# Attention's values product with v held and the probabilities moved, in an early-fusion block

## What is computed

```
q = rope(X @ Wq + bq);  k = rope(X @ Wk + bk);  v = X @ Wv + bv      # 12 heads of 16
scores = einsum('bqhd,bkhd->bhqk', qh, kh) / sqrt(16), causal mask
weights = softmax(scores)
out = einsum('bhqk,bkhd->bqhd', weights, vh).reshape(B, 48, 192)
return out @ Wo + bo
```

## Time and profile before

| | us |
|---|---|
| median of 3 runs | 270.15 (269.02 to 271.35) |
| profiled execution | 271.69 |
| its span in the trace | 268.7 |
| PE busy | 243.2 (91%) |
| DVE busy | 171.9 (64%) |
| ACT busy | 131.2 (49%) |
| POOL busy | 120.2 (45%) |

### The profile page before, as it was taken

How to read it: one execution, slowest core, us unless ns; L and a number is a source line. 1 busy time by engine, 2 the same in 40 slices (tenths; PEclk the granted TensorE clock), 3 DMA queues, 4 the chain that set the end, 5 groups by cost and what they waited for, 6 DMA issues and landing times.

```text
span 268.7 us, 5694 instructions
## 1 busy us (share of the span) xinstructions
PE 243.2 (91%) x2077; PEld 195.3 (73%) x2082; DVE 171.9 (64%) x534; ACT 131.2 (49%) x349; POOL 120.2 (45%) x132
## 2 busy tenths in 40 slices
PE   7887979999899989999989999999999999999920
PEld 2656666666677667667558989899998989898910
DVE  7467349879887977878765585574828293763310
ACT  0214374878597767765345455352717172541300
POOL 8055212451675276342652064462808172647380
PEclk9999999999999999999999999999999999999975
DMA  7960089700001211263014977757585768432241
GB/s 226 357 209 2 1 192 324 324 2 4 32 33 34 99 39 33 69 180 91 32 47 107 271 168 157 171 133 179 82 216 76 178 139 177 91 33 27 27 41 14
DMA packets 24491, 31.03 MB, mean 115 GB/s; under 512 B 3149, under 2 KB 21521, under 8 KB 24336
## 3 DMA queue, kind: packets, MB, share of 16 engines
q1 hardware_dynamic: 16928, 20.77, 28.5%
q0 software_dynamic: 5904, 8.48, 15.8%
q10 hardware_dynamic: 1632, 1.42, 1.9%
HBM read 20.34 MB, written 10.08 MB: 113 GB/s over the span
## 4 chain that ended last, share of the span: by engine, by line
PE 59%; DVE 12%; DMA 8%; issue 6%; POOL 6%; ACT 5%; ACTq 1%; POOLq 0%; SPq 0%; DVEq 0%
PE bank L718 12%; PE scores L709 5%; PE scores L702 5%; PE scores L703 5%; PE scores L710 5%; PE scores L706 4%; PE bank L421 3%; DMA slots<-rows,slot 2%; PE bank L407 2%; PE bank L687 2%; POOL slots L1382 2%; PE bank L492 2%; PE bank L443 2%; DMA early<-in_patches 2%; DMA keys<-slots 2%
## 5 line engine op out<-in xcount | busy, mean ns | idle before, releaser
L1431 POOL DMA_INDIRECT out_rows<-blank,tok x32 | 55.0, 1718 | 63.4 <-DVE blank L1309 56.4
L932 ACT ACTIVATE blank<-scores 128x480 f32<-128x480 f32 (+1 forms) x33 | 18.4, 560 | 58.8 <-PE scores L710 58.8
L1382 POOL DMA_INDIRECT slots<-rows,slot x24 | 24.6, 1024 | 32.7 <-DVE rows L1186 12.0
L718 PE MATMUL bank<-w_sb,blank 128*120 128x192 f32 x224 | 37.7, 326 | 0.0
L718 PEld LDWEIGHTS bank<-w_sb,blank 128*120 128x120 f32 x224 | 36.2, 183 | 0.1
L1320 DVE TENSOR_TENSOR blank<-blank,scores 128x480 f32<-128x480 f32 (+1 forms) x33 | 21.0, 639 | 19.3 <-ACT blank L932 19.2
L1309 DVE SCALAR_TENSOR_TENSOR blank<-bank,keys,blank 120x192 f32<-120x192 f32 x32 | 11.5, 412 | 28.5 <-DMA out_rows<-blank,tok 22.8
L702 PE MATMUL scores<-z0h,wah 128*128 128x480 f32 x64 | 25.4, 397 | 0.0
L709 PE MATMUL scores<-z,wbh 128*128 128x480 f32 x64 | 24.5, 383 | 0.3 <-DVE z L1305 0.3
L703 PE MATMUL scores<-z0h,wal 128*128 128x480 f32 x64 | 24.3, 379 | 0.0
L706 PE MATMUL scores<-z0l,wah 128*128 128x480 f32 x64 | 24.3, 379 | 0.0
(11 more groups left out here) (197 smaller groups left out, 532.2 us busy)
## 6 DMA issues: line engine op xcount, KB each, us to landing
early<-in_w SPq DMA_DIRECT2D x8, 512.0 KB, 5.0
early<-in_w SPq DMA_DIRECT2D x16, 256.0 KB, 6.2
w_sb<-in_w SPq DMA_DIRECT2D x8, 384.0 KB, 4.0
slots<-blank POOLq DMA_DIRECT2D x1, 3030.0 KB, 14.0
keys<-slots SPq DMA_DIRECT2D x8, 378.8 KB, 5.1
early<-in_patches SPq DMA_DIRECT2D x1, 1152.0 KB, 9.8
h_all<-in_hinit SPq DMA_DIRECT2D x1, 864.0 KB, 11.1
tokw_all<-in_tokw ACTq DMA_DIRECT2D x1, 576.0 KB, 4.1
```

Of the source, the lines that this page charges most:

```text
L718: mm = pe.matmul(o, hT[:, m, c * CR:(c + 1) * CR], w2_sb[:, par, m, :], start=(m == 0), stop=(m == MH - 1))
L932: act.activation(sg[:, m % 2, cols], up_bank[2 * (m % 2)][:, cols], ACT.Silu).then_inc(s_silu, 1)
L1382: pool.indirect_dma_start(out=slots, out_offset=bass.IndirectOffsetOnAxis(ap=slot[:, 2 * t + k:2 * t + k + 1], axis=0), in_=rows[:, t, :], ...
L1431: pool.indirect_dma_start(out=out, out_offset=bass.IndirectOffsetOnAxis(ap=tok[:, e, c:c + 1], axis=0), in_=yw[:, c, :], in_offset=None, b ...
```

## The change

`values(j)` holds v and moves the probabilities. For each image (48 moved columns) and pair of heads, `vbd` without its ones (128 rows, 32 columns) is held, and the result, 32 features x 48 tokens, goes to partitions 32 (p mod 4) on of bank 6: pairs of heads 0 to 3 in columns 0 to 111, 4 and 5 in columns 128 on. Then eight matmuls hold a block of ones (128 x 32, new tile `ones_sb`) and move `pT`'s 112 columns: they give each token's sum for a head, repeated over the head's 16 partitions, in columns 256 to 511; pairs of heads 4 and 5 are written twice, so that all 128 partitions are filled. `divide(j)` takes the reciprocal of all of these (128 partitions x 4 x 48) and multiplies twice, straight into `oT0` (128 x 96) and `oT1` (64 x 96), and counts `s_oT`. `turn_attention`, `copy_attention`, `att` and their semaphore waits go.

```diff
--- before.py
+++ after.py
@@ -198,13 +198,13 @@
         kk = sb("kk", [P, 2 * P])
         qT_sb = sb("qT_sb", [P, 2 * 3 * GTOK])
         qT = qT_sb[:, :].rearrange("p (a n k) -> p a n k", a=2, n=3)
-        vbd = sb("vbd", [P, 2, 2, HEADS // 2, 2, HD + 1])
+        vbd = sb("vbd", [P, 2, 2, HEADS // 2, 2, HD])
+        ones_sb = sb("ones_sb", [P, 2, HD])
         sm = sb("sm", [P, HEADS * S])
         mx = sb("mx", [P, HEADS])
         pr = sb("pr", [P, 2, HEADS, HALF])
         pT = sb("pT", [P, 2, HEADS // 2, WIDE])
-        rden = sb("rden", [P, HEADS])
-        att = sb("att", [P, 2, D])
+        rden = sb("rden", [P, 4, S])
         oT0 = sb("oT0", [P, 2, GTOK])
         oT1 = sb("oT1", [D1 + 1, 2, GTOK])
         st2 = sb("st2", [P, 6])
@@ -484,19 +484,18 @@
                     t = projected(j)
                     if t is not None:
                         pe.wait_ge(s_lg, t + 1)
-                w = 2 * (HD + 1)
-                for p in range(HEADS // 2):
-                    for two in range(2):
-                        lo = two * HALF
-                        hi = min(lo + HALF, WIDE)
-                        mm = pe.matmul(b6[lo:hi, p * w:(p + 1) * w], pT[:, j % 2, p, lo:hi],
-                                       vbd[:, j % 2, two, p, :, :].rearrange("p a b -> p (a b)"), start=True, stop=True)
+
+                for two in range(2):
+                    lo = two * HALF
+                    for p in range(HEADS // 2):
+                        at, col = 32 * (p % 4), p // 4 * P + lo
+                        pe.matmul(b6[at:at + 32, col:col + S], vbd[:, j % 2, two, p, :, :].rearrange("p a b -> p (a b)"),
+                                  pT[:, j % 2, p, lo:lo + S], start=True, stop=True)
+                for at, col, p in ((0, 2 * P, 0), (32, 2 * P, 1), (64, 2 * P, 2), (96, 2 * P, 3),
+                                   (0, 3 * P, 4), (32, 3 * P, 5), (64, 3 * P, 4), (96, 3 * P, 5)):
+                    mm = pe.matmul(b6[at:at + 32, col:col + WIDE], ones_sb[:, :, :].rearrange("p a b -> p (a b)"),
+                                   pT[:, j % 2, p, :], start=True, stop=True)
                 mm.then_inc(s_pv, 1)
-
-            def turn_attention(j, b6=b6):
-                pe.wait_ge(s_att, j + 1)
-                pe.transpose(b6[:, 0:WIDE], att[0:WIDE, j % 2, 0:D0], ident_sb[0:WIDE, 0:WIDE])
-                pe.transpose(b6[0:D1, P:P + WIDE], att[0:WIDE, j % 2, D0:D], ident_sb[0:WIDE, 0:WIDE]).then_inc(s_ot, 1)
 
             def project(t, b6=b6):
                 pe.wait_ge(s_oT, pairs_for(t))
@@ -617,8 +616,6 @@
                     stay_warm(3, sc[(j - 1) % 2][:, 0, :])
                 if j == NPAIR - 2:
                     stay_warm(2, b7)
-                if back:
-                    turn_attention(j - 1)
                 if i in (0, 3):
                     if j == 0:
                         for n in range(2):
@@ -643,12 +640,10 @@
             positions(3, b4)
             values(z, b7)
             stay_warm(2, sc[0][:, 0, :])
-            turn_attention(a)
             pe.wait_ge(s_posr, 4)
             pe.wait_ge(s_v, 4 * NPAIR)
             open_first()
             project(NT - 2)
-            turn_attention(z, b7)
             pe.wait_ge(s_place1, 1)
             pe.wait_ge(s_zxl, 1)
             for n in range(2):
@@ -808,14 +803,6 @@
                     act.wait_ge(s_pt, 2 * j + r + 1)
                     act.copy(pT[:, j % 2, 3 * r:3 * r + 3, :].rearrange("p a b -> p (a b)"),
                              sc[j % 2][:, r, 0:3 * WIDE]).then_inc(s_pT, 1)
-
-            def copy_attention(j, b6=b6):
-                g, lo = (j // GP) % 2, (j % GP) * 2 * S
-                act.wait_ge(s_ot, j + 1)
-                for o, rows_, at in ((oT0, P, 0), (oT1, D1, P)):
-                    ins = act.copy(o[0:rows_, g, lo:lo + 2 * S].rearrange("p (a b) -> p a b", a=2),
-                                   b6[0:rows_, at:at + 2 * HALF].rearrange("p (a b) -> p a b", a=2)[:, :, 0:S])
-                ins.then_inc(s_oT, 1)
 
             def weight(b):
                 n = len(BATCHES[b])
@@ -869,8 +856,6 @@
                     copy_v(j)
                 if i == 1 and j >= GP:
                     weight(j // GP - 1)
-                if back:
-                    copy_attention(j - 1)
                 if i in (0, 3):
                     copy_v(j)
                 if j == 0:
@@ -892,8 +877,6 @@
             copy_probs(z)
             weight(3)
             late_high(1)
-            copy_attention(a)
-            copy_attention(z, b7)
 
             act.wait_ge(s_first, 16)
             for c in range(CC):
@@ -946,14 +929,15 @@
             dve.memset(xT1[D1:D1 + 1, :, :], 1.0)
             dve.memset(oT1[D1:D1 + 1, :, :], 1.0)
             dve.memset(qp[:, :], 0.0)
+            dve.memset(ones_sb[:, :, :], 0.0)
             dve.memset(vbd[:, :, :, :, :, :], 0.0).then_inc(s_pre, 1)
             dve.memset(count[:, :], 0.0)
             dve.memset(mean_sb[:, :], 1.0 / D)
             dve.memset(every_sb[:, :], 1.0)
             dve.memset(pr[:, :, :, :], 0.0).then_inc(s_ready, 1)
             dve.wait_ge(s_pre, 2)
-            dve.memset(vbd[0:HALF, :, :, :, 0, HD:HD + 1], 1.0)
-            dve.memset(vbd[HALF:P, :, :, :, 1, HD:HD + 1], 1.0)
+            dve.memset(ones_sb[0:HALF, 0, :], 1.0)
+            dve.memset(ones_sb[HALF:P, 1, :], 1.0)
             dve.wait_ge(s_ident, 16)
             dve.tensor_copy(place_sb[:, :].rearrange("p (b s) -> p b s", s=S)[:, :, 0:NPATCH],
                             ident_sb[:, :].rearrange("p (b s) -> p b s", s=NPATCH)).then_inc(s_place, 1)
@@ -1019,14 +1003,16 @@
 
             def divide(j, b6=b6):
                 dve.wait_ge(s_pv, j + 1)
-                o4 = b6[0:WIDE, 0:HEADS * (HD + 1)].rearrange("p (h d) -> p h d", h=HEADS)
-                dve.reciprocal(rden[0:WIDE, :], o4[:, :, HD]).then_inc(s_den, 1)
+                dve.reciprocal(rden[:, :, :], b6[:, 2 * P:4 * P].rearrange("p (a b) -> p a b", b=HALF)[:, :, 0:S]).then_inc(s_den, 1)
                 dve.wait_ge(s_den, j + 1)
-                if j >= 2:
-                    dve.wait_ge(s_ot, j - 1)
-                dve.tensor_tensor(att[0:WIDE, j % 2, :].rearrange("p (h d) -> p h d", h=HEADS), o4[:, :, 0:HD],
-                                  rden[0:WIDE, :].unsqueeze(2).to_broadcast([WIDE, HEADS, HD]),
-                                  ALU.mult).then_inc(s_att, 1)
+                g, lo = (j // GP) % 2, (j % GP) * 2 * S
+                for o, n, at in ((oT0, P, 0), (oT1, D1, P)):
+                    def both(col):
+                        return b6[0:n, col:col + P].rearrange("p (a b) -> p a b", a=2)[:, :, 0:S]
+
+                    out2 = o[0:n, g, lo:lo + 2 * S].rearrange("p (a b) -> p a b", a=2)
+                    ins = dve.tensor_tensor(out2, both(at), rden[0:n, at // HALF:at // HALF + 2, :], ALU.mult)
+                ins.then_inc(s_oT, 1)
 
             steps = [0]
```

## The result

The changed kernel takes **281.44 us** (median of 4 runs, 281.18 to 281.75) against 269.94 for the kernel before (4 runs, 269.02 to 271.35): ratio 1.042, 95% interval 1.037 to 1.047. That is 11.5 us slower; the forecast was 5.9. The profiled execution took 281.65 with a span of 279.8 and a mean granted clock of 0.963, where the one before had 268.7 and 0.982.

A forecast was written before the change was run, and what follows sets the result against it. VectorE and TensorE, both nearly full and handing over to each other, were taken to bound the loop. 3.5 + 1.2 + 0.3 + 0.9 = +5.9 us gave a median of 276.1 us, range 271.5 to 283.

The forecast's parts named there:

- the second: Rival: reciprocal in `divide` at eight columns' time an element, 1.73 us; `divide` +1.59 us, kernel 281 us; chance 0.20.
- the third rival: TensorE's column groups not four at once: two at a time, values 0.55 us longer, kernel 280 us; chance 0.08.
- The reciprocal: In `divide` on VectorE: 192 instead of 12 elements a partition at 6.0 ns each, 1.31 us instead of 229 ns.
- Values and denominators: The 40 TensorE instructions of a pair over four column groups: 0.95 us, 0.06 more than today.
- The first rival: Reciprocal at one column a beat, 0.42 us; `divide` +0.28 us, kernel not slower, 268.4 us; chance 0.12.
- `divide`: Each pair's reciprocal and two products hold VectorE 1.70 us instead of 0.53, +1.17 us a pair.
- `oT` ready: Attention output ready for `project` 1.78 us after the reciprocal starts, 0.33 earlier than today.
- VectorE above 95% busy: Sign of the forecast: VectorE over 95% busy from 43 to 120 us, `project` waiting for its products.
- The walk of the lag: Stretch 34 to 59.5 us: first three divides add 1.17 us each, +3.5; the fourth adds nothing more.
- The full groups: Two groups of four pairs: idle time takes up part of each divide's 1.17 us; +0.6 a group, +1.2 together.
- The end: Stretch 108.9 to 134 us: +0.3 behind the first divide, about 0.3 for each of the last three pairs, +0.9.
- The term that failed: TensorE's granted clock: more idling expected, but nothing counted for a fall of the clock.

The follow-up runs named there:

- experiment 1: Changed kernel with VectorE copying the 192 denominator columns instead of taking their reciprocal (attention not divided): 266.89 us, ratio 0.988 to the kernel before.
- experiment 2: Changed kernel with nine more idle matmuls on TensorE behind the last tile's projection, before the second late placement: 276.53 us, ratio 1.028 to the kernel before.
- experiment 4: Changed kernel with 96 denominator columns by reciprocal and 96 by copy: median 273.21 us in two clusters, 269.65 to 270.93 and 272.98 to 275.77; ratio 1.004.
- experiment 3: Kernel before, with a second reciprocal of 180 columns (scratch to scratch) ahead of its own in `divide`: 280.61, 287.76, 289.1 and 296.19 us, no ratio.

## Why the prediction was right, and which term was missing

The kernel is slower, and for the reason that was forecast: the length of the reciprocal on an engine that was nearly full. The size was right only by the width of the range. The forecast itself was +5.9, between +3 and +8, which ends at about 278 us; 281.44 lies above that, in the part up to 283 where the second and the third rival stood (281 and 280). Neither happened: the reciprocal took 1.35 us, not 1.73, and values and sums took 0.92 us where the third rival had about 1.5. That the time still fell in the range is luck.

**The reciprocal** (forecast 1.31 us): 1352 ns, right to 3%. The long sizes confirm the slope that three short rows gave: 754 ns at 96 columns and 1352 at 192 make (1352 - 754) / 96 = 6.23 ns a column and 156 ns fixed; that line gives 231 ns for 12, and 229 is in the earlier trace rows. The ordinary column is 1.04 ns, so it is six columns' time. The first rival (0.42 us) and the second (1.73 us) both fall; the measured slope decides. The Trainium skill, VectorE: DVE Perf Modes, "Walkthrough: the 8-slice pipeline in each mode", gives the reciprocal a repeat count of eight; the estimate of eight columns' time that the prediction drew from it is above the six measured here.

**Values and denominators** (forecast 0.95 us): 0.92. The four column groups do work at once, and the third rival falls. With turns and copies gone, experiment 1 shows this part as a gain.

**`divide`** (forecast 1.70 us on VectorE): 1.72 from the reciprocal's start to the next instruction (98.03 to 99.75). **`oT` ready** 1.78 us after the start: 1.79. **Who waits**: `project` for VectorE's products, 8.7 us in eleven waits. VectorE above 95% busy: 97.5 and 96.2% in the two groups, though 91% from 42.5 to 59.5.

**The walk of the lag**: forecast 3.5 us at the end of the first stretch, measured 3.3, and the fourth divide added nothing (+3.30 and +3.31), as said. The full groups: forecast +0.6 each, measured +0.9 each (3.3 to 4.2 and 4.2 to 5.1 between the first divides). Part of this is in the working. These are the idle times of VectorE in the kernel before that the earlier trace rows leave out:

```profile
94.19 0.23 DVE L996 TENSOR_SCALAR gx<-bank,std 128x8 f32<-128x8 f32 x1 [0.38 <-PE bank L422]
...
102.48 0.36 DVE L1049 TENSOR_TENSOR h_all<-bank,h_all 128x192 f32<-128x192 f32 x1 [0.64 <-PE bank L505]
...
108.91 0.36 DVE L1049 TENSOR_TENSOR h_all<-bank,h_all 128x192 f32<-128x192 f32 x1 [0.64 <-PE bank L505]
```

With them, 0.38 + 0.65, 0.59 + 0.64 and 0.88 + 0.64 us can take up something behind the second to fourth divide, and at 1.17 a divide the walk is 0.98, 1.12, 1.06 and 0.71 us late, where the prediction has 0.98, 0.96, 0.8 and 0.6. Measured in the second group: 0.91, 1.13, 1.14 and 0.88. The end: forecast +0.3 and +0.9, measured +2.4 up to the second placement (5.1 to 7.5). The last two divides stand nearly back to back on VectorE, at 129.46 and 132.20, and each added its full price: the lag is 5.2, then 6.4, then 7.5 at the placement; the forecast gave them 0.3 each. So the lag at the placement was 7.5 where the sum had 5.9. With the clock kept up (experiment 2) it was 7.1 at the placement and 6.1 at the experts, and 6.45 in the time: about one microsecond is taken up in between, where the prediction let nothing be taken up. The traces show where. VectorE and TensorE in order of time, before, then in experiment 2:

```profile
132.72 0.38 DVE L1116 TENSOR_SCALAR rows<-h_all,mv,pw 128x192 f32<-128x192 f32 x1 [1.39 <-POOL pw L1375]
...
135.48 0.45 PE L536 MATMUL bank<-wbl,wah 128*128 128x480 f32 x1 [0.97 <-DVE wal L1073]
```

```profile
138.37 0.37 DVE L1103 TENSOR_SCALAR rows<-h_all,mv,pw 128x192 f32<-128x192 f32 x1
...
141.56 0.48 PE L535 MATMUL bank<-wbl,wah 128*128 128x480 f32 x1
```

Before, VectorE stood 1.39 us for GpSimd's `pw`, and TensorE 0.97 us for the `wal` that came after it. In experiment 2 both waits are gone, and the third placement starts 6.1 us later than before (141.56 against 135.48), the second 7.1. So 6.45 lies close to the sum of 5.9 partly because two errors work against each other: the lag was larger than forecast, and a microsecond of it was taken up.

**The term that failed**: "TensorE would idle more, but its granted clock was 1.00 even in the stretch where it was busy 6.96 of 8.50 us ... I count nothing for it." In the loop that held, at 22.11 and 22.23 of 24.70 us. It failed in the tail, which I had costed by VectorE's queue alone, never asking how long TensorE would stand there: 2.15 us before the second placement, busy 0.94 and 0.85 in two stretches of 2 us, and half the clock from within that wait on. Measured worth of the missing term: 4.9 us in experiment 2, nearly the whole gap of 5.6 between forecast and result. An average over 8.5 us was the wrong row to bring; the stretches of 2 us around the last handovers are where it shows.

## What to carry to other kernels

Price a moved or widened instruction by the slope of its own kind, from rows of several sizes, and set what it adds beside what its engine has free per iteration: here about a third of an addition showed in the time while VectorE had room, and about all of it beyond. Then follow the late engine past the loop to the next matmuls that wait for it, and read TensorE's busy time there in short stretches: a wait there costs itself and can cost what the clock then takes from the work behind it (it did in the change and in one cluster of experiment 4, not in experiment 1). If an operation is dear on a full engine, price it on the engine with room before giving up the rest of the change.

## What the runs showed of the hardware

- Reciprocal on VectorE costs 156 ns + 6.23 ns a column, from PSUM and, within 0.3%, from SBUF (1274 ns at 180 columns, the line gives 1277). Right behind the 180 columns in experiment 3, the 12 columns took 169 ns instead of 229. A copy of 192 columns takes 355 ns.
- After the fall in the tail TensorE was busy 2.00 of 2.00 us in every stretch from 138 to 148 and the granted clock stayed at 0.50 throughout; in experiment 4, with the same work behind the break, it was 0.50 from 132 to 134, 0.86 from 134 to 136 and 1.00 from then on. How long it stays down wasn't settled; executions of experiment 4's kernel spread over 6.1 us (269.65 to 275.77), which shrank to 1.9 with the wait filled.
- The Trainium skill, TensorE: Matmul & The Clock Gate, "HAM oscillation — how this bites in real kernels", describes a kernel that loses the clock again in every turn of its loop, where TensorE's work is shorter than its wait for the next transfer. Here it fell once, behind a loop at full clock, in a wait of 2.15 us for VectorE; with that wait filled it did not fall.
